# First cross attention of a two-layer perceiver block: the context turned by VectorE in blocks that ride with the probabilities' DMAs, normalised by GpSimd

## What is computed

```
keys   = values = concat(layer_norm(context) * g1 + b1, layer_norm(latents) * g2 + b2)   # (128, 257 + 32, 128)
scores = (latents A_h) keys^T * 64 ** -0.5          # A_h = Wq_h Wk_h^T, for each of 16 heads
prob   = softmax(where(kept, scores, -big))
x     += sum over heads of (prob values) U_h        # U_h = Wv_h Wout_h
```

## Time and profile before

| | |
|---|---|
| median of 3 runs | 2136.58 us (2135.96 to 2137.06) |
| the profiled execution | 2138.08 us, its span 2136.3 us |
| PE busy | 1820.2 us (85%) |
| DVE busy | 1632.1 us (76%) |
| ACT busy | 1538.9 us (72%) |
| POOL busy | 904.2 us (42%) |
| mean granted TensorE clock | 0.919 of full speed |
| the first cross attention | from about 70 us to about 895 us of the span |

### The profile page before, as it was taken

One profiled execution on the slowest core, in us unless ns is written; L12 is line 12 of the kernel. 1 busy time (PEld: TensorE's weight loads), 2 busy tenths in 40 slices (PEclk: granted clock), 3 DMA queues, 4 the chain that ended last, 5 costly groups with the idle time before them and its releaser, 6 DMA issues. The chain is left out here.

```text
span 2136.3 us, 53459 instructions
## 1 busy us (share of the span) xinstructions
PE 1820.2 (85%) x14283; PEld 1481.1 (69%) x14283; DVE 1632.1 (76%) x5154; ACT 1538.9 (72%) x4185; POOL 904.2 (42%) x1339
## 2 busy tenths in 40 slices
PE   3699999999999999735305899999999899759997
PEld 2599999999999999614202577777777566426775
DVE  5788888888888888466886588888888788735664
ACT  3488888878888887564763688888888688545553
POOL 1544444444444444041560233333333277344554
PEclk8699999999999999966757899999999999879999
DMA  4367777776777776400000222222222000014222
GB/s 138 91 161 164 160 163 164 159 165 154 165 161 161 163 162 153 89 0 0 0 0 0 77 71 68 69 63 74 60 73 65 16 1 0 2 32 102 83 90 83
DMA packets 176775, 192.39 MB, mean 90 GB/s; under 512 B 22064, under 2 KB 154640, under 8 KB 176576
## 3 DMA queue, kind: packets, MB, share of 16 engines
q1 hardware_dynamic: 175222, 189.41, 36.6%
q10 hardware_dynamic: 1194, 1.58, 0.3%
q0 software_dynamic: 288, 0.56, 0.1%
HBM read 86.09 MB, written 4.72 MB: 43 GB/s over the span
## 5 line engine op out<-in xcount | busy, mean ns | idle before, releaser
L1681 ACT ACTIVATE b_prob<-b_neg,b_nmax 128x257 f32<-128x257 f32 x512 | 255.2, 500 | 71.4 <-DVE b_nmax L1628 71.3
L777 ACT ACTIVATE a_prob<-a_neg,a_nmax 128x289 f32<-128x289 f32 x512 | 266.6, 525 | 1.5 <-DVE a_nmax L704 1.2
L839 PE MATMUL a_out<-a_probT,a_xn 128*128 128x256 f32 x1024 | 263.5, 381 | 4.0 <-DMA a_probT<-a_blocks 2.4
L670 POOL TENSOR_TENSOR a_xn<-a_z,g 128x256 f32<-128x256 f32 x128 | 93.5, 731 | 385.3 <-DVE a_z L738 385.3
L829 PE MATMUL a_score<-a_xnT,a_qT 128*128 128x290 f32 x1536 | 253.3, 314 | 2.6 <-DVE a_qT L749 2.6
L704 DVE CUSTOM_DVE_ANT_0 a_neg<-a_score,a_bias 128x289 f32<-128x289 f32 x512 | 211.4, 457 | 40.7 <-PE a_score L829 36.1
L1628 DVE CUSTOM_DVE_ANT_0 b_neg<-b_score,b_bias 128x257 f32<-128x257 f32 x512 | 196.0, 421 | 50.9 <-PE b_score L1724 48.8
L785 ACT ACTIVATE a_prob<-a_prob,a_rinv 128x289 f32<-128x289 f32 x512 | 231.3, 527 | 1.8 <-DVE a_rinv L754 1.7
L829 PEld LDWEIGHTS a_score<-a_xnT,a_qT 128*128 128x128 f32 x1536 | 222.6, 191 | 9.7 <-issue 3.4
L839 PEld LDWEIGHTS a_out<-a_probT,a_xn 128*128 128x128 f32 x1024 | 175.5, 191 | 19.0 <-DMA a_probT<-a_blocks 4.5
L1602 POOL TENSOR_TENSOR b_last_part<-b_v_rows,b_prob 128x128 f32<-128x128 f32 x128 | 52.0, 406 | 318.7 <-ACT b_prob L1681 318.7
(11 more groups left out here) (475 smaller groups left out, 4820.2 us busy)
## 6 DMA issues: line engine op xcount, KB each, us to landing
a_probT<-a_blocks SPq DMA_DIRECT2D x512, 192.0 KB, 3.6
a_raw<-in_ctx SPq DMA_DIRECT2D x128, 128.0 KB, 2.9
b_raw<-in_ctx SPq DMA_DIRECT2D x128, 128.0 KB, 3.3
m_wide<-expert_weights SPq DMA_DIRECT2D x128, 128.0 KB, 2.9
a_kept<-keep SPq DMA_DIRECT2D x32, 257.0 KB, 3.3
b_kept<-keep SPq DMA_DIRECT2D x32, 257.0 KB, 3.6
b_v_rows<-ctx_tail_values SPq DMA_DIRECT2D x32, 256.0 KB, 3.5
latents_normalised<-lat_affine SPq DMA_DIRECT2D x8, 256.0 KB, 2.3
```

The source lines that it names most:

```text
L777: nc.scalar.activation(prob[:, par, grp, 0:KEYS0], neg[:, grp, :], ACT.Exp, bias=nmax[:, par, grp:grp + 1], scale=-1.0, accum_out=rsum[:, ...
L839: nc.tensor.matmul(out_ps[:, half, 0:2 * P], xn[:, j, kt, :], probT[:, u, 2 * half:2 * half + 2, kt, :], start=(kt == 0), stop=False)
L1681: nc.scalar.activation(prob[:, n, grp, :], neg[:, par, grp, :], ACT.Exp, bias=nmax[:, par, grp:grp + 1], scale=-1.0, accum_out=rsum[:, n, ...
```

## The change

The normalised context is no longer turned by PE. POOL now writes `xn` whole: it subtracts the mean and multiplies with rstd (two instructions of 128x128), then the product with g1 and the sum with b1, in place. DVE's normalisation and the tile `z` are gone. DVE turns `xn` in 32x32 blocks into 64 further columns of `blocks` (448 instead of 384), the four DMAs of each step carry these columns along into `probT`, and ACT and DVE make the high and low half from `probT` instead of from PSUM.

The batches that a step works on move too: statistics s+8 instead of s+7, normalisation s+7, block turning s+6, and the two halves s+4 instead of s+5. ACT's high half stands at the head of its step and waits for the DMAs of `probT`; DVE's low half stays at the end of its step. SP's `spread_prob` waits for that low half (`xnT_ready` at s+5) besides what it waited for. POOL waits for `out_ready` at s before it writes `xn`. `LEAD` is 8, and the last 16 steps are peeled instead of 8. The score's own wait (`xnT_ready` at s+4, L823) is unchanged.

```diff
-def run_steps(eng, step, lead, lag=0):
+def run_steps(eng, step, lead, lag=0, rest=8):
...
-        LEAD, LAG = 7, 1
+        LEAD, LAG, REST = 8, 1, 16
...
-            return (g * 4 + (j // 2 + 1)) * 64
+            return (g * 4 + (j // 2 + 3)) * 64
+
+        def probs(n, kt, half):
+
+            return probT[:, n, 2 * half:2 * half + 2, kt * P:(kt + 1) * P]
+
+        def carried_ctx(j):
+
+            return probT[:, j % 2, :, KEY_TILES * P:].rearrange("p i (k m) -> p k i m", k=2 * KEY_STEP)
+
+        def ctx_cols(j, half):
+
+            return xnT[:, half, (j + 4) % 8, 0:2 * P].rearrange("p (k i m) -> p k i m", k=2 * KEY_STEP, i=4)
...
-                def load_raw(g, j):
-                    sp.dma_start(raw[:, j % 4], io["ctx_1024"][ds(g * 8 + j, 1), 0:2 * P, :].rearrange(
+                def load_raw(b, j):
+                    sp.dma_start(raw[:, j % 4], io["ctx_1024"][ds(b, 1), 0:2 * P, :].rearrange(
...
-                    wait_apart(k, sp, blocks_ready, s + 3)
+                    wait_apart(k, sp, blocks_ready, s + 7)
+                    if live(g, j, 4):
+                        wait_apart(k, sp, xnT_ready, s + 5)
                     wait(sp, out_ready, s + 1)
                     for i in range(4):
-                        heads = slice(i * L, (i + 1) * L)
-                        sp.dma_start(probT[:, n, i].rearrange("p t q -> p (t q)"),
-                                     blocks[heads, n].rearrange("c r t g l -> c r (t g l)")).then_inc(probT_loaded[n], 16)
+                        sp.dma_start(probT[:, n, i], blocks[i * L:(i + 1) * L, n]).then_inc(probT_loaded[n], 16)
...
-                    if live(g, j, 8):
-                        if live(g, j, 4):
-                            wait_apart(k, sp, z_ready, s + 5)
-                        load_raw(g + 1, j)
+                    if live(g, j, 9):
+                        if live(g, j, 5):
+                            wait_apart(k, sp, z_ready, s + 6)
+                        load_raw(s + 9, j + 1)
...
-                    if live(g, j, 2):
+                    if live(g, j, 2) or live(g, j, 6):
                         spread_prob(g, j)
...
-                    if live(g, j, 6):
-                        n, par = (j + 6) % 8, j % 2
-                        pool.wait_ge(z_ready, s + 7)
-                        nc.gpsimd.tensor_tensor(xn[:, n], z[:, par], spread(k.g1), ALU.mult).then_inc(scaled, 1)
-                        pool.wait_ge(scaled, s + 7)
+                    if live(g, j, 7):
+                        n, par = (j + 7) % 8, (j + 1) % 2
+                        wait(pool, out_ready, s)
+                        wait_apart(k, pool, rstd_ready, s + 8)
+                        for kt in range(2):
+                            last = nc.gpsimd.tensor_scalar(xn[:, n, kt, :], raw[:, (j + 7) % 4, kt, :], mv[:, par, kt, 0:1],
+                                                           rstd[:, par, kt:kt + 1], ALU.subtract, ALU.mult)
+                        last.then_inc(z_ready, 1)
+                        pool.wait_ge(z_ready, s + 8)
+                        nc.gpsimd.tensor_tensor(xn[:, n], xn[:, n], spread(k.g1), ALU.mult).then_inc(scaled, 1)
+                        pool.wait_ge(scaled, s + 8)
                         nc.gpsimd.tensor_tensor(xn[:, n], xn[:, n], spread(k.b1), ALU.add).then_inc(xn_ready, 1)
-                    if live(g, j, 7):
-                        par = (j + 1) % 2
-                        wait_apart(k, pool, mv_ready, s + 8)
+                    if live(g, j, 8):
+                        par = j % 2
...
-                    dve.wait_ge(prob_ready, s + 3)
-                    if live(g, j, 0):
+                    if live(g, j, 4) or live(g, j, 2):
                         dve.wait_ge(probT_loaded[n], probT_loads(g, j))
-                    nc.vector.transpose(blocks[:, n, :, 0:2].rearrange("p r t g l -> p g r t l"),
-                                        prob[:, n, :, 0:2 * P].rearrange("p g (r t c) -> p g r t c", t=2, c=L))
-                    nc.vector.transpose(blocks[:, n, 0:2, 2].rearrange("p r g l -> p g r l"),
-                                        prob[:, n, :, 2 * P:2 * P + 2 * L].rearrange("p g (r c) -> p g r c", c=L)).then_inc(blocks_ready, 1)
+                    if live(g, j, 6):
+                        dve.wait_ge(xn_ready, s + 7)
+                        last = nc.vector.transpose(blocks[:, n, :, KEY_TILES * P:].rearrange("p f (r t m) -> p t f m r", r=KEY_STEP, t=2),
+                                                   xn[:, (j + 6) % 8].rearrange("p t (c f) -> p t f c", f=KEY_STEP))
+                    if live(g, j, 2):
+                        dve.wait_ge(prob_ready, s + 3)
+                        nc.vector.transpose(blocks[:, n, :, 0:2 * P].rearrange("p r (t g l) -> p g r t l", t=2, l=L),
+                                            prob[:, n, :, 0:2 * P].rearrange("p g (r t c) -> p g r t c", t=2, c=L))
+                        last = nc.vector.transpose(blocks[:, n, 0:2, 2 * P:3 * P].rearrange("p r (g l) -> p g r l", l=L),
+                                                   prob[:, n, :, 2 * P:2 * P + 2 * L].rearrange("p g (r c) -> p g r c", c=L))
+                    last.then_inc(blocks_ready, 1)
...
-                    if live(g, j, 2):
+                    if live(g, j, 2) or live(g, j, 6):
...
-                    if live(g, j, 7):
-                        n, par = (j + 7) % 4, (j + 1) % 2
...
-                    if live(g, j, 6):
-                        n, par = (j + 6) % 4, j % 2
-                        dve.wait_ge(rstd_ready, s + 7)
-                        wait(dve, xn_ready, s + 5)
-                        for kt in range(2):
-                            last = nc.vector.tensor_scalar(z[:, par, kt, :], raw[:, n, kt, :], mv[:, par, kt, 0:1],
-                                                           rstd[:, par, kt:kt + 1], ALU.subtract, ALU.mult)
-                        last.then_inc(z_ready, 1)
-                    if live(g, j, 7):
-                        par = (j + 1) % 2
-                        wait_apart(k, dve, stats_ready, s + 8)
+                    if live(g, j, 8):
+                        par = j % 2
+                        wait(dve, z_ready, s + 7)
+                        wait_apart(k, dve, stats_ready, s + 9)
...
-                    if live(g, j, 5):
-                        dve.wait_ge(xnT_hi, s + 6)
-                        n = (j + 5) % 8
-                        nc.vector.tensor_tensor(xnT[:, LO, n, 0:2 * P], ctx_ps[:, 0:2 * P], xnT[:, HI, n, 0:2 * P],
-                                                ALU.subtract).then_inc(xnT_ready, 1)
+                    if live(g, j, 4):
+                        dve.wait_ge(xnT_hi, s + 5)
+                        nc.vector.tensor_tensor(ctx_cols(j, LO), carried_ctx(j), ctx_cols(j, HI), ALU.subtract).then_inc(xnT_ready, 1)
...
+                    if live(g, j, 4):
+                        act.wait_ge(probT_loaded[j % 2], probT_loads(g, j))
+                        nc.scalar.activation(ctx_cols(j, HI), carried_ctx(j), ACT.Copy).then_inc(xnT_hi, 1)
...
-                    if live(g, j, 5):
-                        act.wait_ge(ctx_turned, s + 6)
-                        nc.scalar.activation(xnT[:, HI, (j + 5) % 8, 0:2 * P], ctx_ps[:, 0:2 * P], ACT.Copy).then_inc(xnT_hi, 1)
...
-                        wait(pe, xnT_ready, s + 5 if live(g, j, 4) else B)
+                        wait(pe, x_added, t - 1)
...
-                    if live(g, j, 5):
-                        n = (j + 5) % 8
-                        pe.wait_ge(xn_ready, s + 6)
-                        wait(pe, xnT_ready, s + 5)
-                        if b == 0:
-                            wait(pe, x_added, t)
-                        for kt in range(2):
-                            last = nc.tensor.transpose(key_order(ctx_ps[:, 0:2 * P], kt), xn[:, n, kt, :], k.ident[:])
-                        last.then_inc(ctx_turned, 1)
```

More of the change, by code:

```diff
@@ L428, in wait_apart @@
     eng.sem_inc(k.passed, 1)
-def run_steps(eng, step, lead, lag=0):
+def run_steps(eng, step, lead, lag=0, rest=8):
     for s in range(-lead, 8):
         step(s // 8, s % 8)
-    with eng.Fori(1, B // 8 - 1) as g:
+    with eng.Fori(1, (B - rest) // 8) as g:
         for j in range(8):
             step(g, j)
-    for s in range(B - 8, B + lag):
+    for s in range(B - rest, B + lag):
         step(s // 8, s % 8)
@@ L565, in xattn0 @@
         prob = sb("a_prob", [P, 2, GROUPS, (N_BLOCKS + 2) * L])
-        blocks = sb("a_blocks", [P, 2, KEY_STEP, KEY_TILES, GROUPS, L])
-        probT = sb("a_probT", [P, 2, 4, KEY_TILES, P])
+        blocks = sb("a_blocks", [P, 2, KEY_STEP, KEY_TILES * P + 2 * L])
+        probT = sb("a_probT", [P, 2, 4, KEY_TILES * P + 2 * L])
         rsum, rinv = sb("a_rsum", [P, 2, GROUPS]), sb("a_rinv", [P, 2, GROUPS])
@@ L644, in step @@
                             .then_inc(tail_loaded[u], 16)
-                for j in range(8 - LEAD):
-                    load_raw(0, j)
```

(14 more changed lines are left out.)

16 lines of the change are left out of this document (9 added, 7 removed).

## The result

The change makes the kernel slower: **2271.01 us** (2266.18 to 2272.13, 4 runs) against 2136.82 us (2135.96 to 2138.28, 4 runs) on the same chip, a ratio of 1.0623 with a 95% interval of 1.0604 to 1.0641. That is 134 us more; 104 were forecast, and the time lies inside the range (2208 to 2286).

The account below looks back on a forecast made before the run. PE was taken to bound the kernel, and with the change PE and DVE to run in turn. Tiles of 28.1 us for 24.88 added 100, the start 4: 2241 us, range 2208 to 2286.

Parts of the forecast that it names:

- PE and DVE in turn: Scores wait for DVE's low half from the step before, in three steps of four: 6.21 us per step instead of 5.32.
- second loop: From SP's refill of probT to the low half, over two steps: 12.7 us against 12.4 for two laps.
- lap: One DVE step, 5.14 us from first mask to low half, plus 1.07 to the next first mask: 6.21 us.
- context transpose: DVE's new block transpose of 256 elements: 0.33 us taken, like L717, with 1.16 as the bound from above.
- Statistics and aggregate: DVE's two instructions L731 and L745 within its step, taken at 0.36 and 0.20 us.
- My sum for that rule: With the skill's DMA estimate, 2.5 us for 224 KB, the second loop never decides: 2217 us.
- PE's own part: Two transposes per batch go from PE: plain step 5.10 us, step with projection 8.70, 28 us possible gain.
- The sum: Tile 28.1 us instead of 24.88, 31 times: +100; start +4, end nothing; median 2241 us.
- POOL's instruction: Two more POOL instructions of 128x128, at most 0.44 us each by L688, 0.9 per step, hidden.
- Rival 1: DVE's low half, with both inputs from SBUF, collides with POOL's rstd: 2272 to 2288 us, chance 0.20.
- Rival 2: PE's granted clock falls with PE busy 85% of a tile: some 80 us more, 2300 and above, chance 0.06.
- Rivals 3 and 4: Faster, DVE's lap fits into PE's: 2109 us, chance 0.04; low half ready in time: 2109 to 2137, chance 0.02.

Follow-up runs that it names:

- one-step-late kernel: The kernel before, with the context's PE transposes, high half and low half made for batch s+4 instead of s+5, nothing else: 2224.96 us, ratio 1.0407.
- the kernel whose context does not ride: The changed kernel with its four DMAs carrying only the 384 probability columns (192 KB instead of 224), context columns left zero: 2251.52 us, ratio 1.0529.
- first low-half version: The changed kernel with DVE's context low half moved from the step's end to right behind the masks: 2192.34 us, ratio 1.0255.
- queries last: The changed kernel with low half behind the masks, ACT's output copy before its high half, and PE's queries behind all values: 2186.60 us, ratio 1.0232.
- the kernel with this part alone: The kernel before, with the normalised context made by POOL instead of DVE and nothing else: 2140.63 us, ratio 1.0013.
- the reordered versions: Changed kernel, low half behind masks: 2192.34 us; also ACT's output copy before its high half: 2175.60; also PE's queries behind the first values: 2140.73.
- the two best versions: Changed kernel, low half early, output copy first; queries behind first values: 2140.73 us; or last, but before values in projection steps, with split clearing: 2141.10.

## Why the prediction was right, and where it was off

**The mechanism held, and the code of the waits gave it.** PE and DVE in turn, in three steps of four, with ACT's high half released by the DMAs and the second loop deciding only in b = 2: all of it stands in the rows above. The one-step-late kernel shows the turn without a ride, the kernel whose context does not ride shows the second loop by its absence. By my own list of signs: DVE's low half releases the scores in three steps of four (yes), a lap near 6.2 (6.47), the first mask waiting 0.5 to 1.1 us in every step (0.99 at b = 2 and 1.00 at b = 3, but 2.19 behind the projection), ACT's high half at b = 2 near 0.5 behind PE's start (0.71; it waits for the DMAs in every step, not only there), POOL near 15 us per tile and not waited for (18.1, but not waited for).

**The lap was mis-sized by 0.26 us.** Its terms, in the step shown:
- The context transpose was taken at 0.33 on the path, like L717. It takes 0.60 there (441.77 to 442.37), 0.68 alone. The same number of elements was not the same instruction. This is the largest miss, +0.27 per lap. The bound from above, 1.16, did contain it.
- Statistics and aggregate were 0.36 + 0.20; they are 0.76 (443.82 to 444.58). In the kernel before the two normalisations stood between them. With these gone the aggregate waits 0.15 for the statistics' result, a stall that had been covered: +0.20 in all.
- The other way: masks 1.60 for 1.68, L735 1.12 for 1.16, the low half and the handoff to PE 0.53 for 0.65; the way from PE's start to the mask is 0.85 for 0.81. Together -0.20.

**Second loop:** from b = 2 to b = 3 the forecast had 6.9 us (13.1 - 6.21) against 6.2 for a lap; measured are 7.13 against 6.43 (the lap without the context's bytes): 0.7 in both. This agreement is partly luck. The ride of b = 2 took 6.89 us (439.61 to 446.50) in place of 6.2, which alone would have made the excess 1.3; but two of DVE's own laps came 0.6 later too, and what counts is the difference. The landing took 4.2 us for 224 KB, 0.6 more than the earlier trace rows, and the ride grew by 0.70 with the bytes (6.03 to 6.73, medians): the upper bound of 0.7, and not the 0.3 that I took. By the Trainium skill's rule that I set against it (DMA: Bandwidth & Descriptors, section Anatomy of one DMA — SWDGE (gpsimd) path) the estimate for one of these DMAs is 2.5 us. That section is about DMAs that GpSimd issues, these come from SP's queue, and for them the measured 4.2 decides. (My sum for that rule was off as well: a second loop that never decides takes 0.65 us off each of 31 tiles, which gives 2221 and not 2217.)

**PE's own part** was right: the step with projection took 8.58 where I had 8.70, and PE's plain step, where nothing held it, was 5.10 (first low-half version) to 5.12 us (queries last).

**The sum.** The 31 intervals lost 116.0 us in place of 100: 0.5 x 31 = 15 by the tile, 28.59 for 28.1, and 1 by rounding and the ends of the stage. The start lost 17.8 in place of 4: 8.4 before the first score, and 9.4 from there to the first projection, since the seven steps ahead of it run in turn too, and in part at the lower clock. My sum took whole tiles from the first projection on and forgot them. 16 and 14 are the 30 us that were missing.

**POOL's instruction** of 128x128 was bounded by L688, 0.44; L681 took 0.80. That bound was too low by nearly a factor of two. 18 us of POOL per tile in place of 15 did no harm, since PE and DVE never waited for it in the steady state; the kernel with this part alone, whose tile is as long as before, agrees.

**Rival 1, the collision with POOL,** did not happen where I put it. The low half L775 ran beside rstd (445.26 inside 445.18 to 445.90) and took 0.40 us. In the reordered versions the same instruction met a POOL instruction that reads 128x1024 elements and took 1.28. The Trainium skill, SBUF — State Buffer, section Who interferes with whom, has a VectorE instruction with two SBUF inputs and a reading GpSimd one exclude each other for the whole instruction. With the bias instruction the trace agrees (the low half ended 0.27 after POOL's), and with the product with g1 (0.72 us, ended 0.28 after POOL's). With rstd, two elements per partition in 0.72 us, it does not, nor with POOL's normalisation L681: in the version with the low half early it lay wholly inside one of these 0.80 us instructions and took 0.42. What sets them apart no run here shows. My reading of the earlier trace rows was also too kind: of the eight instructions only the one of 1007 ns began while POOL was at work, so the median of 688 said little against the rival. **Rival 2:** in the tiles the clock stayed at 1.00 of full speed, the 2.4 GHz level, with PE busy 24.74 of 28.72 us. Its sign did appear at the start (107.4 to 121.0 and 172.2 to 175.6 us), where it cost a few us and not the rival's 80. **Rivals 3 and 4** fell with the row of PE's waits for L775.

**What stays open.** PE without its transposes should need 5.10 x 3 + 8.70 = 24.0 us per tile, and the two best versions stay at 24.5 and 24.6 although PE shows busy nearly all the time. Of that, waits of its weight loads for `probT` are 0.3 to 0.4 per tile (9.3 and 10.2 us in 680); that they carry over to PE in full is not shown. The remaining 0.2 was not traced.

## What to carry to other kernels

- Before the instructions of a moved step are counted, write down for each engine of which batch it now writes what the others read, and in which of its steps. If a result made at the end of a step is wanted at the head of the next one, two engines that overlapped will run in turn; here that alone cost 87 us in the kernel before, against 28 that the saving could have brought.
- A saving on the bounding engine is worth what the next one leaves: with every order mended, PE's 28 us shrank to 4.5 over the 31 intervals and were eaten by a start that was 7.25 longer.
- An instruction of the same size is not a price. Where pattern or operands differ, carry the wide bounds into the sum; and when instructions between a producer and its reader go, count the stall that they covered.

## What the runs showed of the hardware

- A transpose of 128x256 f32 in 32x32 blocks took 0.40 us as L737 and 0.68 us as L731; with neighbouring columns read, 0.62.
- GpSimd's tensor_scalar of 128x128 f32 with two scalars per partition takes 0.80 us, more than its 128x256 tensor_tensor with 0.73 (L685).
- Four DMAs of 192 KB each from SBUF to SBUF behind each other land after 3.6 us, of 224 KB after 4.2: 0.6 us for 17% more bytes. From the first issue to the last landing it is 6.0 and 6.7.
- Two instructions that both read SBUF on DVE (two inputs, 128x256) and POOL ran side by side in some cases (0.40 us beside rstd, 0.42 inside a tensor_scalar of 128x128), and DVE's waited in others (1.28 beside a tensor_scalar of 128x1024, 0.72 and 0.93 beside a tensor_tensor of 128x256).
